# The matrix engine's two step loops: heads placed on a fetch block, back edges announced

## The reference

```
x = x + linear_attention(layernorm(x))
x = x + ffn(layernorm(x))            # 6 layers
x = x + retention(layernorm(x))
x = x + ffn(layernorm(x))            # the same 6 layers, the same weights

def ffn(x):
    for i in range(6):
        x = attn_layer(shift_tokens(x), Wqkv[i], ...) + x     # local attention, 16 heads
        x = ffn_layer(shift_tokens(x), ln_g[i], ...) + x      # gated, 128 -> 341 -> 128
    return x
```

## Time and profile before

| | us |
|---|---|
| median of 3 runs | 3267.62 |
| lowest and highest | 3261.32 and 3268.75 |
| the profiled execution's own time | 3268.94 |
| its span, first to last instruction | 3267.1 |
| PE busy | 2997.5 (92%) |
| DVE busy | 2863.2 (88%) |
| ACT busy | 2279.6 (70%) |
| POOL busy | 1791.3 (55%) |

### The profile page before, as it was taken

How to read it: one execution, slowest core, us unless ns; L and a number is a source line. 1 busy time by engine, 2 the same in 40 slices (tenths; PEclk the granted TensorE clock), 3 DMA queues, 4 the chain that set the end, 5 groups by cost and what they waited for, 6 DMA issues and landing times.

```text
span 3267.1 us, 93385 instructions
## 1 busy us (share of the span) xinstructions
PE 2997.5 (92%) x37658; PEld 1884.2 (58%) x37896; DVE 2863.2 (88%) x2671; ACT 2279.6 (70%) x3707; POOL 1791.3 (55%) x823
## 2 busy tenths in 40 slices
PE   8689998999899998999999999999999999999997
PEld 4355555555555555555566655665665665665563
DVE  5688888888888888888999989999999999999995
ACT  4467676667667676667666777777777777777774
POOL 8555554555555555555454556655655655555551
PEclk9899999999999999999999999999999999999998
DMA  9544544544444454455344445445445445445442
GB/s 318 167 110 100 141 113 101 136 107 110 112 126 107 105 141 106 104 135 137 87 120 106 103 102 146 114 109 146 113 110 146 112 109 148 111 109 149 112 116 65
DMA packets 254585, 400.99 MB, mean 123 GB/s; under 512 B 51148, under 2 KB 84872, under 8 KB 254280
## 3 DMA queue, kind: packets, MB, share of 16 engines
q1 hardware_dynamic: 254280, 396.41, 46.5%
HBM read 64.64 MB, written 19.92 MB: 26 GB/s over the span
## 4 chain that ended last, share of the span: by engine, by line
PE 40%; DVE 24%; ACT 19%; issue 12%; POOL 1%; SPq 1%; DVEq 0%; DMA 0%; ACTq 0%; POOLq 0%
PE ps L842 6%; PE ps L860 5%; PE ps L800 5%; PE ps L876 5%; PE ps L821 4%; PE ps L781 4%; ACT f_ab L1088 4%; DVE f_mx L1356 4%; DVE f_p L1359 3%; ACT f_u L1087 3%; PE ps L782 3%; PE ps L783 3%; DVE f_p L1371 3%; ACT ps L1099 3%; ACT f_p L1105 3%
## 5 line engine op out<-in xcount | busy, mean ns | idle before, releaser
L1285 POOL TENSOR_TENSOR f_w<-f_w,f_ab 128x1024 f32<-128x1024 f32 x192 | 549.1, 2860 | 527.1 <-DVE f_w L1336 527.1
L1290 POOL TENSOR_TENSOR f_ab<-f_w,f_rn 128x1024 f32<-128x1024 f32 x192 | 595.4, 3101 | 418.5 <-DVE f_rn L1346 410.0
L1281 POOL TENSOR_TENSOR f_u<-f_u 128x512 f32<-128x512 f32 x384 | 570.4, 1498 | 458.7 <-ACT f_u L1087 445.7
L1087 ACT ACTIVATE f_u<-ps 128x512 f32<-128x512 f32 x768 | 466.7, 608 | 183.6 <-PE ps L783 148.5
L1336 DVE TENSOR_TENSOR f_w<-f_ab,f_tan 128x1024 f32<-128x1024 f32 x384 | 494.4, 1328 | 71.4 <-ACT f_ab L1088 69.1
L1088 ACT ACTIVATE f_ab<-ps,f_pa 128x512 f32<-128x512 f32 x768 | 541.2, 705 | 1.2
L781 PE MATMUL ps<-f_xh,f_wh 128*128 128x512 f32 x768 | 395.1, 514 | 149.5 <-issue 82.3
L842 PEld LDWEIGHTS ps<-f_tb,f_v 128*64 128x64 f32 x6144 | 395.8, 137 | 109.9 <-issue 75.7
L842 PE MATMUL ps<-f_tb,f_v 128*64 128x160 f32 (+1 forms) x6144 | 441.9, 297 | 17.1 <-DMA f_tb<-f_pt 13.5
L1099 ACT ACTIVATE ps<-ps 128x512 f32<-128x512 f32 x384 | 204.7, 574 | 346.8 <-PE ps L800 346.4
L860 PE MATMUL ps<-f_ot,f_wout 128*128 128x512 f32 x768 | 367.2, 601 | 10.0 <-issue 6.7
(11 more groups left out here) (164 smaller groups left out, 4760.7 us busy)
## 6 DMA issues: line engine op xcount, KB each, us to landing
f_kb<-f_ab SPq DMA_DIRECT2D x384, 256.0 KB, 3.6
f_qb<-f_ab SPq DMA_DIRECT2D x384, 256.0 KB, 3.6
f_tb<-f_pt SPq DMA_DIRECT2D x1344, 64.0 KB
f_wh<-split_w SPq DMA_DIRECT2D x48, 384.0 KB, 4.4
f_wl<-split_w SPq DMA_DIRECT2D x48, 384.0 KB, 4.2
a_w_raw<-wqkv SPq DMA_DIRECT2D x24, 384.0 KB, 4.7
split_w<-a_w_hi SPq DMA_DIRECT2D x24, 384.0 KB, 4.6
split_w<-a_w_lo SPq DMA_DIRECT2D x24, 384.0 KB, 5.6
```

The lines of the kernel that those rows point to most:

```text
L1087: nc.scalar.activation(u[:, i, :], bank("qk", g, i), ACT.Square).then_inc(sq_done.sem, 1)
L1281: nc.gpsimd.tensor_tensor(u[:, 2 * i + 1, :], u[:, 2 * i, :], u[:, 2 * i + 1, :], ALU.add).then_inc(sq_sum[i].sem, 1)
L1285: nc.gpsimd.tensor_tensor(w[:, 0:2, :], w[:, 0:2, :], ab[:, k % 2, 0:2, :], ALU.add).then_inc(q_sum.sem, 1)
L1290: nc.gpsimd.tensor_tensor(ab[:, k % 2, 0:2, :], w[:, 0:2, :], rn[:, 0:1, :].broadcast_to([128, 2, N]), ALU.mult).then_inc(rope_q.sem, 1)
```

## The change

A helper `loop` opens the two loops. For every engine but PE it is the loop of before.

```
+                def loop(eng, first, end):
+                    if eng.engine != mybir.EngineType.PE:
+                        return eng.Fori(first, end)
+
+                    return nc.Fori(first, end, engines=bass.OrderedEngineSet([eng.engine]), hint_back_edge=True, head_slot={eng.engine: 0})
+
                 def steps_of(eng, step):
 
                     step(0, False, True)
-                    with eng.Fori(1, RET1) as s:
+                    with loop(eng, 1, RET1) as s:
                         step(s, True, True)
                     for s in range(RET1, RET2 + B):
                         step(s, True, True)
-                    with eng.Fori(RET2 + B, STEPS - B + 1) as s:
+                    with loop(eng, RET2 + B, STEPS - B + 1) as s:
                         step(s, True, True)
```

## The result

The changed kernel takes 3168.31 us (median of 4 runs, 3165.03 to 3171.00) against 3267.68 of the kernel before beside it (3261.32 to 3268.75). The ratio is 0.9699, with a 95% interval of 0.9683 to 0.9716: faster by 3.0%. The forecast was 3166.

A forecast was written before the change was run, and what follows sets the result against it. The prediction took a PE–DVE hand-over as the bound, with PE's first-loop fetch stalls on the path: 3268.94 − 102.7 (placement) + 0.4 (padding) + 0 (hint) = 3166.6 us, 3166 at the median; range 3156 to 3190.

The forecast's parts named there:

- The placement term: PE's first loop: heads on slot 0 save 20 stalls, 102.7 us; the second loop gains nothing.
- a count of blocks: PE's instruction fetch: with nine blocks going round nothing is kept, with one block fewer all is kept.
- The padding: Ahead of each PE loop: one taken branch to the next block, +0.4 us, at most 10.3 for both.
- The hint at no cost: One instruction in each of 39 PE iterations: 0 to 9.3 us in all, hidden, so taken as 0.
- its cover: At L806 in the second loop: PE's sequencer is ready 0.6 us before DVE's release, which hides the hint.
- The two parts of the stall: First loop, per step: 3.53 us less wait before L781 (70.6 in all) and 1.60 us of slow clock (32).
- the body might stay on nine blocks: Rival, first loop: the loaded program is shifted against the blocks, all 20 stalls remain, 3269 us; chance 0.05.
- The slower rival: Both PE loops: the hinted block takes its own place, the second loop gets stalls too, 3356 us; chance 0.04.
- a falling clock: Rival: waits of 0.59 us at each head keep the slow stretches, only idle time returns, 3199 us; chance 0.04.
- small prices paid: Rival: both padding branches miss (10.3 us) and every hint is paid (9.3 us), 3186 us; chance 0.05.

The follow-up runs named there:

- slots 0, 180, 181: Changed kernel without the hint, heads of both PE loops on that slot of a block: 3169.34, 3167.33 and 3165.95 us.
- slot 230: Changed kernel without the hint, heads of both PE loops on slot 230, 50 instructions in an eighth block: 3219.15 us, ratio 0.9849.
- slot 190: Changed kernel without the hint, heads of both PE loops on slot 190, ten instructions in an eighth block: 3177.04 us, ratio 0.9702.

## Why the prediction was right

**The placement term held.** 102.7 us were forecast from 66.58 − 61.45 us per step, and 102.7 us went; that they agree to the tenth is closer than runs of one kernel agree with each other. What carried it was that the second loop had the same body and showed the state after the change, with its idle time and its clock, so that nothing of the stall had to be modelled.

**Its reading, a count of blocks, held**, and the experiments sharpen it: eight stay, nine do not, and the ninth is the block behind the loop. The Trainium skill ("Advanced Engine Details and Errata", section "ISA Cache") gives 128 KB in lines of 16 KB, by which, as the prediction estimated, there are eight, and the table above agrees. The same section says that there are only two lines, and the Trainium skill's "Runtime: NRT & Kernel Launch", section "Instruction fetch mechanics", has a window of two pages. Neither fits PE's back edge here: with seven and with eight blocks in the body (slots 0, 180, 181 and the hint alone) it took 0.21 to 0.28 us and nothing was fetched after the first pass.

**The padding**, forecast at 0.4 us with a ceiling of 10.3, is 0.326 + 0.421 = 0.75 us of branch. The ceiling was not idle: in the run with 120 idle instructions the branch ahead of the second loop took 3.6 us, and a fetch began 1.0 us after it.

```profile
L575 PEldq COMPARE_BRANCH  x19: 76/208/3615, 2032.7 to 3335.0; - x19
```

**The hint at no cost** was right, and its cover was undersized: "0.6 us before DVE releases it" came from taking the 3.2 us behind the branch as something that stays. They were a second fetch. The cover is 3.6 us (the run with 70 idle instructions), against 0.031 us for the hint.

**The two parts of the stall** were sized rightly, 3.53 us of idle time and 1.60 us of slow clock. From the start of the branch to PE's first load the 20 back edges took 7.51 us on the mean before and 4.02 at the median after, 3.49 less, which leaves 1.64 of the 5.13 to the clock. The idle instructions make a like pair, 4.0 and 1.7. What I had wrong is where the idle time came from. I took it for the 4.1 us of the branch. The first fetch alone would have been hidden but for 0.4 us (slot 230, on the mean); it was the second, caused by a head on the last slots of its block, that PE stood still for.

**What the hint does** was the weakest point. I gave it no share in the gain, and left open that the body might stay on nine blocks in spite of it, for 3269 us. The run with the hint alone shows that this rival was all but impossible: with the hint the ninth block is not fetched. The slower rival, a second copy of the head, fell with the same run. The rivals of a falling clock (3199) and of small prices paid (3186) fell with the clock of 1.00 and the 0.75 us above. Not settled is why the time up to the first loop varies by 7 us between runs of such kernels.

## What to carry to other kernels

Read each hardware loop from back edge to back edge, and hold loops with equal bodies against each other: here the difference between them was one of address, and it could be had back. A compare and branch of 4 us and fetches on the instruction queue in every iteration are its signs, but what it costs is what the engine stands idle for behind it, with the clock that falls; here a sequencer that was 3.6 us ahead hid nearly the whole of one fetch, and nothing of a second. The hint is the sturdier cure (it also served a body of twice the size), while a placement holds only as long as the body leaves next to nothing in the eighth block (1 instruction did no harm, 10 did), and a gain of 3% that four harmless instructions also bring should make one careful with any measured effect of an edit ahead of a long loop.

## What the runs showed of the hardware

- Instructions came in blocks of 16.4 KB; PE kept eight and lost all in turn with nine (0, 6 and 31 stalled back edges of 37 with 1, 10 and 50 instructions in the eighth).
- A taken branch on PE to a block that was there took 0.21 to 0.28 us in the loop and 0.19 to 0.42 over the padding; to one that was not, 3.4 to 5.2 us, and 3.6 over the padding once (120 idle instructions).
- At a head whose second instruction lay in the next block, and neither block was there, PE waited twice, 4.1 and 3.2 us.
- A hint took 31 ns and replaced the fetch of the block behind the loop; for a body of 3,223 instructions it cut the branch from 3.7 to 2.1 us.
- A wait that is long fulfilled, in a row of such, takes 0.109 us on PE's sequencer, its record 0.051.
- Behind 4 us of idle time in the loop PE's granted clock read 0.50, the 1.2 GHz level, with a fetch (the kernel before) and without (70 idle instructions). At slot 230, with waits of up to 1.8 us, it read 1.00 through both loops; at slot 190 it read 0.50 for 3.4 us behind one wait of 1.6 us (423.4 to 426.8) and 1.00 behind another of 1.8.
